# Routing part of a two-layer attention and expert kernel: the turn of the next batch's rows goes between the halves of u, its low part ahead of the routing's steps, and the last full step takes the order of the others

## The reference, cut to what matters

```
x = x + attention_a(layernorm(x))      # Nystrom attention, 16 heads
x = x + ffn(layernorm(x))              # routing part and experts, run 0
x = x + attention_b(layernorm(x))      # causal attention with rotary positions
x = x + ffn(layernorm(x))              # routing part and experts, run 1

def ffn(x):
    xln = ln(x, ln1)
    att = sigmoid(xln @ Wr) * (xln @ Wv) @ Wo
    state = xln @ Ws
    x = x + att
    h = ln(x, ln2)
    conf = sigmoid([h @ conf_rwkv.T, h @ conf_trans])          # 3 numbers a token
    bids = conf * capital_shares * sigmoid(h @ w_diff) + h @ W_aff
    winner = argmax(bids)
    coef = conf[winner] / (conf[winner] + 1e-6)
    out_e = square(relu(h @ K[e])) @ V[e]                      # experts 0 and 1
    out_2 = ((h @ W1) * sigmoid(state @ W2)) @ W3              # expert 2
    return x + out[winner] * coef
```

## Time and profile before

| | us |
|---|---|
| median of three runs | 2378.61 |
| profiled execution | 2377.76 |
| its span | 2375.7 |
| PE busy | 2176.4 (92%) |
| DVE busy | 1491.8 (63%) |
| ACT busy | 1027.3 (43%) |
| POOL busy | 676.3 (28%) |
| routing part, run 0 | about 953 to 1197 |
| routing part, run 1 | about 1937 to 2163 |

### The profile page before, as it was taken

How to read it: one execution, slowest core, us unless ns; L and a number is a source line. 1 busy time by engine, 2 the same in 40 slices (tenths; PEclk the granted TensorE clock), 3 DMA queues, 4 the chain that set the end, 5 groups by cost and what they waited for, 6 DMA issues and landing times. The chain is left out here.

```text
span 2375.7 us, 50326 instructions
## 1 busy us (share of the span) xinstructions
PE 2176.4 (92%) x19611; PEld 1762.4 (74%) x19611; DVE 1491.8 (63%) x3888; ACT 1027.3 (43%) x1986; POOL 676.3 (28%) x768
## 2 busy tenths in 40 slices
PE   7799999999999999898799986899998988988998
PEld 7688888888888888777689973454554557767998
DVE  2565665747565564688656656777777628875665
ACT  4343434333443433444245531555555543433554
POOL 3210110101010100466522223333334115662222
PEclk8899999999999999999999996999999989999999
DMA  7300000000000000421657756555545235114775
GB/s 242 121 19 11 10 10 11 19 2 19 11 10 11 11 2 2 135 64 62 240 168 225 226 148 120 99 89 94 92 83 82 43 98 203 37 45 133 224 224 140
DMA packets 156100, 212.87 MB, mean 90 GB/s; under 512 B 51848, under 2 KB 140192, under 8 KB 150560
## 3 DMA queue, kind: packets, MB, share of 16 engines
q1 hardware_dynamic: 141420, 190.73, 28.3%
q0 software_dynamic: 12864, 17.38, 4.4%
q10 hardware_dynamic: 1584, 1.57, 0.3%
HBM read 141.93 MB, written 67.69 MB: 88 GB/s over the span
## 5 line engine op out<-in xcount | busy, mean ns | idle before, releaser
L2447 DVE CUSTOM_DVE_ANT_0 bank<-bank,b_raw_masks 128x512 f32<-128x512 f32 (+3 forms) x512 | 239.2, 518 | 123.0 <-PE bank L2682 116.0
L2572 ACT ACTIVATE b_probsT<-bank 128x512 f32<-128x512 f32 x320 | 181.0, 603 | 167.6 <-PE bank L2682 136.8
L2161 PE MATMUL bank<-e_hT_hi,k_rwkv 128*128 128x256 f32 x1088 | 221.3, 287 | 2.8 <-DVE e_hT_lo L2065 2.8
L2161 PEld LDWEIGHTS bank<-e_hT_hi,k_rwkv 128*128 128x128 f32 x1088 | 179.7, 193 | 3.3 <-DVE e_hT_lo L2065 3.3
L796 POOL TENSOR_TENSOR probs<-probs,rcp 128x512 f32<-128x512 f32 x64 | 66.9, 1045 | 345.5 <-DVE rcp L665 345.5
L2682 PE MATMUL bank<-b_k_stacked,b_q_stacked 96*128 96x512 bf16 (+3 forms) x512 | 129.5, 317 | 33.8 <-DVE b_neg_max L2447 24.2
L2161 PE MATMUL bank<-e_hT_lo,k_rwkv 128*128 128x256 f32 x544 | 154.5, 284 | 0.0
L2175 PE MATMUL bank<-v_rwkv_hi,e_hidden_hi 128*128 (+1 forms) x544 | 152.8, 281 | 0.4 <-DVE e_hidden_lo L2086 0.4
L2175 PE MATMUL bank<-v_rwkv_lo,e_hidden_hi 128*128 (+1 forms) x544 | 152.3, 280 | 0.0
L2175 PE MATMUL bank<-v_rwkv_hi,e_hidden_lo 128*128 (+1 forms) x544 | 152.2, 280 | 0.0
L2122 ACT ACTIVATE e_relu<-bank,k_bias 128x256 f32<-128x256 f32 x272 | 113.6, 470 | 77.3 <-PE bank L2161 74.3
(11 more groups left out here) (362 smaller groups left out, 6128.9 us busy)
## 6 DMA issues: line engine op xcount, KB each, us to landing
k_rwkv<-scratch_k SPq DMA_DIRECT2D x32, 2048.0 KB, 7.3
scratch_b_parts<-b_part SPq DMA_DIRECT2D x93, 128.0 KB, 2.5
b_q_stacked<-scratch_b_parts SPq DMA_DIRECT2D x90, 128.0 KB, 4.3
b_k_stacked<-scratch_b_parts SPq DMA_DIRECT2D x90, 128.0 KB, 4.4
rows<-scratch_rows SPq DMA_DIRECT2D x34, 258.0 KB, 7.9
scratch_rows<-rows SPq DMA_DIRECT2D x16, 516.0 KB, 7.9
x_tokens<-in_x_dram SPq DMA_DIRECT2D x8, 512.0 KB, 7.2
scratch_x_out<-x_tokens SPq DMA_DIRECT2D x8, 512.0 KB, 3.4
```

Of the source, the lines that this page charges most:

```text
L2161: last = nc.tensor.matmul(data[:, half * ROWS:(half + 1) * ROWS], ff.k_part(i % 2, a)[:, k, at:at + P], hT[b][:, i % 2, k], start=n == 0, ...
L2447: last = nc.vector.tensor_tensor_reduce(data[:, at:at + size], data[:, at:at + size], raw_masks[:, T - size:T], -1.0, LARGEST, ALU.add, AL ...
L2572: nc.scalar.activation(probsT[:, ring, u], fl.data("st", pair, u)[:], ACT.Exp, scale=DB ** -0.5).then_inc(fl.released("st", pair, u), 1)
```

## The change

On PE, the turn of xT for batch j + 1 stood after attention and now stands between the two halves of u. On ACT, the copies to f_xT_hi move ahead of those of f_gt, and the sigmoid f_sig stands between the two halves of f_tT_hi. On DVE, the low part of xT goes ahead of the logits, and the second half of f_gt between the logits and the routing's chain. Step 7 loses its own branch on DVE, ACT and PE and takes the same order (with no turn of xT, as there is no batch 8); in it DVE normalises rows ahead of `add_third`, and POOL makes f_tT_lo ahead of `second_deviation`. The list of PSUM fills follows.

```diff
         order += pair("hT", m) if j else []
-        if j == B - 1:
-            order += [("route", m), ("routeT", m)] + pair("att", j) + pair("s", j) + pair("u", m)
-        elif j == B:
+        if j == B:
             order += [("route", m), ("u", m, 0), ("routeT", m), ("u", m, 1), ("rank", m)] + pair("w3", m)
         else:
             order += pair("s", j)
-            order += [("route", m)] + pair("u", m) + [("routeT", m)] if j else []
+            order += [("route", m), ("u", m, 0)] if j else []
+            order += pair("xT", j + 1) if j + 1 < B else []
+            order += [("u", m, 1), ("routeT", m)] if j else []
             order += pair("att", j)
-            order += pair("xT", j + 1)
...
-            def gated_third(m):
+            def gated_third(m, outs=range(CT)):
                 ready((s["t_lo"], m * CT))
-                for k in range(CT):
+                for k in outs:
...
@@ vector
-                if j == B - 1:
-                    logits_of(m)
-                    route(m)
-                    first_sum(j)
-                    second_statistics(j)
-                    gated_third(m)
-                    second_normalise(j)
-                    add_third(m)
-                    place(m)
...
                 else:
                     if m >= 0:
-                        gated_third(m)
+                        gated_third(m, (0,))
+                    if j + 1 < B:
+                        turned_lo(j + 1)
+                    if m >= 0:
                         logits_of(m)
+                        gated_third(m, (1,))
                         route(m)
                     first_sum(j)
-                    turned_lo(j + 1)
                     second_statistics(j)
+                    if j == B - 1:
+                        second_normalise(j)
                     if m >= 0:
                         add_third(m)
                         place(m)
-                    second_normalise(j)
+                    if j < B - 1:
+                        second_normalise(j)
@@ gpsimd
                 if j == B - 1:
+                    second_part(gt, tT, "t_hi", "t_lo", m)
                     second_deviation(j)
-                    second_part(gt, tT, "t_hi", "t_lo", m)
@@ scalar
-                if j >= B - 1:
+                if j == B:
                     turned_logits()
                     confidences()
-                    if j < B:
-                        second_gate()
                     third()
                 else:
                     second_gate()
                     if m >= 0:
                         turned_logits()
-                        third()
+                    if j + 1 < B:
+                        for k in range(CT):
+                            first_part(("xT", j + 1, k), xT[0][:, k], "xT_hi")
+                    if m >= 0:
+                        third((0,))
                         confidences()
-                if j + 1 < B:
-                    for k in range(CT):
-                        first_part(("xT", j + 1, k), xT[0][:, k], "xT_hi")
+                        third((1,))
@@ tensor
-                if j == B - 1:
-                    route()
-                    turn_logits()
-                    attention()
-                    to_features(("s", j), "WsW2", xT)
-                    to_features(("u", m), "W1", hT)
-                    third()
-                    rank()
...
-                        to_features(("u", m), "W1", hT)
+                        to_features(("u", m), "W1", hT, (0,))
+                    if j + 1 < B:
+                        pe.wait_ge(s["xq_done"], (j + 2) * TT)
+                        turn(("xT", j + 1), lambda t, k: xq[:, t, k * P:(k + 1) * P])
+                    if m >= 0:
+                        to_features(("u", m), "W1", hT, (1,))
                         turn_logits()
                     attention()
-                    pe.wait_ge(s["xq_done"], (j + 2) * TT)
-                    turn(("xT", j + 1), lambda t, k: xq[:, t, k * P:(k + 1) * P])
                     if m >= 0:
                         third()
                         rank()
```

More of the change, by code:

```diff
@@ L1770, in confidences, with third @@
                     nc.scalar.activation(sig[:], logits[:, :, 0:4], ACT.Sigmoid).then_inc(s["sig_done"], 1)
-                def third():
-                    for k in range(CT):
+                def third(outs=range(CT)):
+                    for k in outs:
                         act.wait_ge(*read("u", m, k))
                         nc.scalar.activation(tT[0][:, k], gt[:, k], ACT.Copy).then_inc(s["t_hi"], 1)
-                if j >= B - 1:
+                if j == B:
                     turned_logits()
                     confidences()
-                    if j < B:
-                        second_gate()
                     third()
```

## The result

| | before | after |
|---|---|---|
| median, us | 2379.42 (5 runs, 2374.04 to 2383.83) | 2360.82 (5 runs, 2358.66 to 2366.78) |
| ratio | | 0.9914 (0.9893 to 0.9935) |
| profiled execution, us | 2377.76 | 2366.78 |
| routing part, run 0, r(0) to route(8) | 211.73 | 206.21 |
| routing part, run 1, r(0) to route(8) | 195.83 | 180.90 |

The change takes 18.6 us off the median (0.9% by the ratio; 15 to 25 us by its interval), where 14.4 were forecast. By the prediction's bound of 0.5% it is faster. The profiled execution of after was the slowest of its five runs. Its routing parts are 20.4 us shorter than before's, its total only 11.0. The stretches that the change doesn't touch took the rest: route(8) of run 0 to r(0) of run 1 is 777.2 us there against 770.4, and r(0) of run 0 comes 3.8 us later. A second execution of the changed kernel has 774.1 for the former.

The account below looks back on a forecast made before the run. DVE was taken to bound the routing steps. Gains of 2.1 + 4.8 (run 0) and 5.2 + 4.7 (run 1) make 16.8 us; less 2.4 for the clock, 14.4 off 2378.6 gives 2364 us, range 2353 to 2374.

Parts of the forecast that it names:

- The bound: Routing steps: DVE's own sum, working or held for some 22 of 24.28 us, counts; not PE's gap of 2.3 us.
- The walk of the middle step: Steps 1 to 5, retimed from step 5 of run 1: no f_sig wait, one chain instruction held 1.2 us.
- The size of the middle step: Steps 1 to 5: gain 0.95 us a step, giving steps of 23.3 us.
- just hidden: Middle step, POOL: four scatters (5 us) end at 2086.3, when f_var's input comes, so they cost nothing.
- The edges: Steps 0 and 6: step 0 gains 0.8 us (run 0) and 0.3 (run 1), step 6 gains 0.15.
- The weight steps: Run 0, steps 2 to 5: PE-bound steps 2 and 3 lose 0.9 and 0.75 us; 4 and 5 gain 0.9 each.
- rival A: Only last full steps gain; elsewhere DVE waits for logits that PE brings late: 9.5 us, 2369 us, chance 0.20.
- The clock term: PE's clock falls after waits in two steps of twelve, 1.56 us each, less 1.2 slack: 2.4 us deducted.
- The last step: Step 7, the last full step: PE's waits are filled; gain 4.7 us in run 1, 4.8 in run 0.
- B: Rival: POOL's hold on the chain goes too and the clock stays up: 2352 us, chance 0.10.
- C: Rival: POOL becomes the chain through f_tT_lo, scatters, f_var, f_both; middle steps gain nothing: 5 us, 2373 us, chance 0.08.
- D: Slower rival: xT's turn waits for f_xq, logits late, clock falls twice; middle steps lose 2.75 us: 2401 us, chance 0.07.

Follow-up runs that it names:

- run 0: Not a follow-up: the first of the kernel's two routing parts, 953 to 1197 us in the profile before; r(0) to route(8) 211.73 us before, 206.21 after.
- run 1: Not a follow-up: the second of the kernel's two routing parts, 1937 to 2163 us in the profile before; r(0) to route(8) 195.83 us before, 180.90 after.
- experiment 8: Changed kernel with u whole before xT's turn (run 0, steps 2 to 5) and two of four scatters ahead of f_tT_lo: 2361.32 us, 0.9911.
- Experiment 3: Kernel before, steps 0 to 6: f_sig and logits between the halves of f_gt and f_tT_hi, xT's turn still late: 2382.78 us beside 2383.16.
- experiment 6: Changed kernel, but POOL's second f_tT_lo waits for the end of the routing's chain: 4132.72 us; run again, 2395.8 us beside 2381.96 of before.
- again: Second execution of the changed kernel, no edit: 2363.17 us, 0.9929 against the kernel before.
- third: Third execution of the changed kernel, no edit: 2364.85 us, 0.9928 against the kernel before.
- experiments 7: Changed kernel, but in run 0's steps 2 to 5 PE does u whole before the turn of xT: 2365.7 us, 0.9933 against the kernel before.

## Why the prediction was right, and where its sizes were off

**The bound.** PE isn't the bound: in after it still waits 2.5 us a step (1.73 for rows, 0.26 for f_xq, 0.50 for f_tT_lo). That DVE's own sum sets the whole step is too wide. From the end of rows to the end of f_mv it does (19.19 us in before, 17.96 in after, nearly without gaps). From f_mv to the end of rows it takes 5.09 us in both, and there POOL's f_var, f_rstd and addition are the chain (experiment 8). Experiment 3 shows that the wait for f_sig by itself is worth nothing; experiment 6 takes 1.2 us out of the chain, but its steps are longer, so it says nothing on the bound.

**The walk of the middle step** held in each point named but the step's length: r follows rank at once, 1.73 us of wait before the turn of hT, no wait for f_sig, L1449 and L1450 under 0.2 us. One instruction is held, f_win, for 1.29 us: the one that the prediction calls L1454 and that is L1453 in after. The Trainium skill (SBUF — State Buffer, "Who interferes with whom") says that a VectorE instruction with two SBUF inputs contends with a GpSimd instruction that reads SBUF, and that one with at most one SBUF input, outside the two-port modes, doesn't. The trace agrees: beside the first f_tT_lo (2052.13 to 2053.43) the logits' addition and the second half of f_gt, which each read a bank, take 0.17 and 0.73 us; beside the second f_win takes 1.29. The prediction named f_gt of before for this, and there it proves nothing: f_gt ends at 2077.75, and f_tT_lo begins at 2077.84. That a reduce slips through isn't tested: L1452 begins at 2053.91, takes 0.17 us and is over as the second f_tT_lo begins.

**The size of the middle step.** Forecast 0.95 us, measured 1.25 (24.28 to 23.03). This term was sized too small. The chain is 4.43 us and not 4.6: without its hold it takes 3.23 (experiment 6), where 3.39 was worked out. It also starts 0.14 us earlier than walked, since DVE's instructions overlap a little in the trace. rows takes 1.70 us and not 2.13 (its row in before's trace: 2066.12, 2.13), because it starts later against POOL's addition; that it starts later is the new wait of 0.65 us for the scatters, which the prediction didn't have. It had "just hidden" only for f_var. Experiment 8 shows that the two cancel.

**The edges.** By r, step 0 of run 1 gained 1.4 to 1.5 us at the same clock, where 0.3 was forecast, and step 1 0.5 for 0.95. That is the mark and not the work. In "again" r(1) no longer waits for f_xT_lo; before's row is first:

```profile
1964.63 0.19 PEld L1816 LDWEIGHTS bank<-f_xT_hi,wr_ff_hi 128*128 128x128 f32 x1 [1.83 <-DVE f_xT_lo L1397]
```

```profile
1960.38 0.19 PEld L1812 LDWEIGHTS bank<-f_xT_hi,wr_ff_hi 128*128 128x128 f32 x1
```

By the end of rows on DVE the intervals are these (us, run 1; "0" is from r(0), "last" from the end of rows in step 6 to route(8)):

| | 0 | 1 | 2 | 3 | 4 | 5 | 6 | last |
|---|---|---|---|---|---|---|---|---|
| before | 23.18 | 24.38 | 24.30 | 24.31 | 24.30 | 24.29 | 22.53 | 28.54 |
| again | 22.81 | 23.33 | 22.98 | 23.04 | 23.03 | 23.04 | 21.76 | 23.43 |
| forecast gain | 0.3 | 0.95 | 0.95 | 0.95 | 0.95 | 0.95 | 0.15 | 4.7 |
| gain | 0.37 | 1.05 | 1.32 | 1.27 | 1.27 | 1.25 | 0.77 | 5.11 |

So step 0 came as forecast; in run 0 it gained 0.6, 0.8 and 1.3 us in three executions for 0.8. Step 6 was mis-sized: DVE waits there 0.26 us for the logits and not 0.7.

**The weight steps.** Forecast: steps 2 and 3 bound by PE, a loss of 0.9 and 0.75. Measured by r: 2.1 to 2.8 and 0.7 to 2.0. In step 2 the way from rows to w3 grew by 1.6 to 2.0 us; with u whole on PE, where PE waits less and its clock stays up, it grew by 0.7, near the walk's 0.9. Here rival A's mechanism is seen. This is DVE of after in step 2 of run 0:

```profile
1028.01 1.37 DVE L1414 TENSOR_SCALAR f_xq<-x_tokens,f_mv,f_both 128x256 f32<-128x256 f32 x4
...
1033.80 0.19 DVE L1432 TENSOR_TENSOR f_logits<-bank,bias_ff 128x32 f32<-128x32 f32 x1 [1.00 <-PE bank L1906]
```

and PE there, by weight loads and by stretch:

```profile
1029.44 1.57 PEld L1829 LDWEIGHTS bank<-ident,f_xq 128*128 128x128 f32 x8 [2.77 <-DVE f_xq L1414]
```

```profile
1026.50:1033.30 6.80, 4.47 (x17) 3.39 (x15) 6.30 (x16) 2.48 (x5) 1.17 (x2) 0.75 0.01 4
```

PE stands for f_xq (the prediction's 2.7 us, there for step 5), and behind the wait its clock is down: its 8 turns take 1.57 us instead of 0.86, and the logits come 1.0 us late. In step 5 the wait is the same, the turns take 0.85, and the clock is down behind them (0.76 from 1111.00 to 1118.00; logits 0.67 late). The same wait doesn't always do it: in the three executions the clock is down in five of these six steps, and in step 5 of "third" it stays at 1.00 behind 2.79 us, and DVE waits for nothing. In steps 3 and 4 of after the waits are 1.30 and 1.09 us, the turns take 0.86, and DVE waits for nothing. Step 4 gave 1.7 us back, and run 0 up to step 7 came out at 0.6 to 2.4 us for 2.1 forecast. That this range holds the forecast is luck: by the end of rows the four weight steps lost 0.7 to 2.3 us where the forecast had a gain of 0.15, and steps 1 and 6 gave more than forecast (1.1 for 0.95 and 0.75 for 0.15).

**The clock term.** 2.4 us were taken off for falls in two steps of twelve, from a slow r pass that costs 1.53 us by the earlier trace rows (4.21 less 2.68), not 1.56. In run 1 each of the steps 1 to 5 agrees within 0.1 us in three executions, so none shows one. The falls came in run 0's weight steps, which were walked at full clock: steps 2 and 3 lost together 2.8 to 4.5 us for 1.65 forecast. Where PE waits longest, for f_xq at 2.8 us, is where the deduction belonged.

**The last step.** Forecast 4.7 and 4.8 us; measured from r(7) 4.73 (34.35 to 29.62) and 4.90 (34.57 to 29.67). The walk started from route at 2118.9 and not from r(7), which comes 0.4 us earlier in after; from the end of rows in step 6 the gains are 5.1 and 5.3. DVE and then PE of after, run 1:

```profile
2120.78 1.15 DVE L1453 TENSOR_TENSOR f_win<-f_bids,f_top 128x12 f32<-128x12 f32 x1
...
2128.47 1.38 DVE L1538 TENSOR_SCALAR rows<-f_x,f_mv,f_rstd 128x256 f32<-128x256 f32 x4 [1.48 <-POOL f_rstd L1658]
```

```profile
2133.82 0.09 PEld L1899 LDWEIGHTS bank<-f_hT_hi,router_hi 128*8 128x8 f32 x1 [2.35 <-DVE f_hT_lo L1396]
```

One hold in the chain but for 0.18 us at L1449, rows without one (2.88 us in the earlier trace rows), f_hT_lo behind add_third and place: as walked. DVE's 0.93 us of wait for the logits are in the walk too. rows takes 1.38 us for the 1.7 walked, which is most of the 0.4 us that came on top.

**In sum**, by the two executions at the ordinary clock of step 0: run 0 gained 7.3 and 6.8 us for 6.9 forecast, run 1 12.4 and 12.3 for 9.9. That is 19.7 and 19.1 us for 14.4. The terms that were mis-sized are, by the end of rows in "again", run 1's 5.2 us up to step 7 (7.3: 1.4 more in steps 1 to 5, 0.6 in step 6, 0.1 in step 0), the last step (0.4 more) and the 2.4 taken off for the clock. Of the rivals, A's mechanism costs something in the weight steps 2 and 5 alone; in steps 6 and 7 DVE waits for the logits too (0.26 and 0.93 us), and the walk had both, the former at 0.7. B falls, since the hold stays. C falls too, since POOL still waits 0.17 us for f_var's input, but by so little that its scatters show on DVE as the wait of 0.65 us. D falls by the steps of 23.0.

## What to carry to other kernels

Where a chain of tiny instructions stands beside a long one of another engine that holds it, look at when the two meet before you look at the wait in front of the chain: taking that wait away gave nothing, and getting half of the long one done ahead was part of 0.8 us a step. A wait moved ahead in a queue also delays what stands behind it there, so work it out again for each kind of step: at 0.3 us it cost nothing, at 2.8 us (the weight steps) PE's clock was down after it in five of six steps, and DVE stood for the logits. And read the changed part by its own marks in the trace, in more than one execution: the total of a single one hid half of the gain here. Choose a mark that the change doesn't move against the bound: by r, step 0 seemed to gain 1.4 us, and by DVE's own work 0.4.

## What the runs showed of the hardware that was not expected

- The granted clock of the same passes (r and v of step 0, run 1) was 1.00 in one execution of the changed kernel and 0.68 in the next: 1.8 us from chance.
- Behind the same wait of 1.94 or 1.95 us in front of w3 (step 2, run 0) the clock was 1.00 in one kernel and 0.60 in another (experiments 7 and 8).
- One execution of a kernel took 4132.72 us, and the next of the same kernel 2395.8. PE's 128x256 matmuls took 445 ns in the former. VectorE's short instructions were not slower, and the records show a granted clock of 1.00.
- A chain of short DVE instructions beside two POOL additions that follow each other without a gap advances one instruction in each addition: 0.61 and 1.20 us in the earlier trace rows, 1.26 and 1.21 in experiment 3, each ending with an addition. In after, beside POOL's scatter issues, which follow f_tT_lo at 2055.5, the same kind of instruction took 0.16 to 0.23 us.
- From the end of the last scatter's issue (2059.48 + 0.96 = 2060.44) to the release of the DVE instruction that waits for its landing (2063.91) it is 3.5 us.
